# A gated cross-attention and ternary feed-forward block: another order of a step, token scales by one transpose, and another beginning

## The reference

```python
x = x + tanh(g_xattn) * attention(layernorm(x), ctx)          # 16 heads of 16, softmax over 128 keys
x = x + tanh(g_ffn) * ffn(layernorm(x))

def ffn(x):                        # D = 256, H = 1024
    h = bit_linear(x, w1)          # tokens rounded to 8 bits by their own maximum, weights ternary
    h = silu(depthwise_conv(h, conv_w, conv_b))   # 3 taps along the sequence, per feature
    return bit_linear(h, w2)
```

## Time and profile before

| | |
|---|---|
| median of 3 runs | 257.64 us (256.51 to 257.85) |
| profiled execution, its own time | 256.99 us |
| its span (first to last instruction) | 255.2 us |
| TensorE matmul busy | 217.7 us, 85% |
| VectorE busy | 200.0 us, 78% |
| ScalarE busy | 148.6 us, 58% |
| GpSimd busy | 123.1 us, 48% |
| mean granted clock of TensorE | 0.957 |

### The profile page before, as it was taken

One profiled execution on the slowest core, in us unless ns is written; L12 is line 12 of the kernel. 1 busy time (PEld: TensorE's weight loads), 2 busy tenths in 40 slices (PEclk: granted clock), 3 DMA queues, 4 the chain that ended last, 5 costly groups with the idle time before them and its releaser, 6 DMA issues.

```text
span 255.2 us, 6530 instructions
## 1 busy us (share of the span) xinstructions
PE 217.7 (85%) x2418; PEld 176.0 (69%) x2418; DVE 200.0 (78%) x414; ACT 148.6 (58%) x261; POOL 123.1 (48%) x227
## 2 busy tenths in 40 slices
PE   7577789889889999999999999989965886776874
PEld 7546677778778787777877877867744665665763
DVE  3123437989888479998988989879899999998971
ACT  0533664537446487676775866766763665666551
POOL 3302012472552747568586584653657524234360
PEclk9955999999999999999999999999995899999998
DMA  6951010110110101101000000000000000101011
GB/s 173 367 182 41 3 44 0 46 44 1 44 35 9 44 1 44 41 3 45 0 23 1 4 3 0 3 3 1 3 1 3 21 32 32 41 21 44 22 63 64
DMA packets 9489, 9.87 MB, mean 39 GB/s; under 512 B 1010, under 2 KB 9202, under 8 KB 9458
## 3 DMA queue, kind: packets, MB, share of 16 engines
q1 hardware_dynamic: 9458, 9.46, 11.5%
HBM read 7.36 MB, written 2.10 MB: 37 GB/s over the span
## 4 chain that ended last, share of the span: by engine, by line
PE 38%; DVE 21%; POOL 20%; issue 15%; ACT 5%; POOLq 0%; DVEq 0%; ACTq 0%
PE ps_score L410 5%; DVE zmax L948 5%; DVE smax L806 4%; POOL hid L310 4%; PE ps_max L420 4%; PE ps_proj L383 4%; PE ps_proj L375 3%; DVE y L862 3%; PE ps_av L434 3%; PE ps_proj L457 3%; DVE hid L855 3%; POOL xn L294 3%; PE ps_av L590 2%; PE ps_av L444 2%; DVE xres L958 2%
## 5 line engine op out<-in xcount | busy, mean ns | idle before, releaser
L806 DVE TENSOR_REDUCE smax<-ps_max 128x8 f32<-128x1024 f32 x32 | 39.2, 1224 | 28.5 <-PE ps_max L420 26.6
L652 ACT ACTIVATE prob<-ps_score 128x1024 f32<-128x1024 f32 x32 | 32.8, 1025 | 21.3 <-PE ps_score L410 20.8
L410 PE MATMUL ps_score<-Qs,KT 32*128 32x128 f32 x512 | 37.1, 282 | 8.2 <-ACT QT L647 6.2
L410 PEld LDWEIGHTS ps_score<-Qs,KT 32*128 32x128 f32 x512 | 31.7, 186 | 16.1 <-issue 15.2
L420 PE MATMUL ps_max<-KT,QT 32*128 32x256 f32 x256 | 38.1, 417 | 1.5 <-DVE smax L806 1.5
L681 ACT ACTIVATE y<-hid,conv 128x512 f32<-128x512 f32 x32 | 26.0, 813 | 7.9 <-DVE hid L855 7.1
L287 POOL TENSOR_SCALAR var<-mv 128x1 f32<-128x1 f32 x16 | 3.6, 224 | 52.5 <-DVE mv L837 52.5
L865 DVE SCALAR_TENSOR_TENSOR y<-hid,conv,y 128x508 f32<-128x508 f32 x32 | 25.5, 797 | 1.1
L862 DVE SCALAR_TENSOR_TENSOR y<-hid,conv,y 128x508 f32<-128x508 f32 x32 | 24.6, 768 | 0.9 <-ACT y L681 0.9
L420 PEld LDWEIGHTS ps_max<-KT,QT 32*128 32x128 f32 x256 | 22.9, 192 | 2.7 <-issue 2.4
L487 PE MATMUL ps_h<-xqT,w1q 128*128 128x512 bf16 x64 | 19.5, 388 | 1.1 <-ACT deq L668 0.7
(11 more groups left out here) (113 smaller groups left out, 519.9 us busy)
## 6 DMA issues: line engine op xcount, KB each, us to landing
cin<-ctxT SPq DMA_DIRECT2D x16, 128.0 KB, 2.1
xres<-x SPq DMA_DIRECT2D x16, 128.0 KB, 2.4
out<-xres SPq DMA_DIRECT2D x16, 128.0 KB, 1.7
w1f<-w1T SPq DMA_DIRECT2D x1, 1024.0 KB, 6.8
w2f<-w2T SPq DMA_DIRECT2D x1, 1024.0 KB, 9.2
wk<-wkT SPq DMA_DIRECT2D x1, 256.0 KB, 2.9
wv<-wvT SPq DMA_DIRECT2D x1, 256.0 KB, 4.2
wq<-wqT SPq DMA_DIRECT2D x1, 256.0 KB, 4.5
```

The lines of the kernel that those rows point to most:

```text
L410: mm = pe.matmul(ps_score[:, i * 512 + j * P:i * 512 + (j + 1) * P], KT[b % 3][rows, j * P:(j + 1) * P], Qs[rows, j * P:(j + 1) * P], star ...
L652: act.activation(prob[pair][:, :], ps_score[:, :], ACT.Exp, scale=DH ** -0.5).then_inc(exp_done, 1)
L806: dve.tensor_reduce(dst, ps_max[:, :].rearrange("p (g t e k) -> p g t e k", g=PG, t=KD, e=2), AX.X, ALU.max).then_inc(max_done, 1)
```

## The change

It has four parts.

1. TensorE's order in a step: `project_v(n)` comes before `weigh(a)` instead of late; `int_transpose` moves from before `weigh` to behind `max_transpose`; `unweighted_transpose(a)` moves behind `project_q(n)`. The column sums of w2 move from step 6 to step 7.
2. Token scales: GpSimd no longer builds `deq_diag`; TensorE transposes the column of scales, read 128 times, and the mean of the weights is multiplied in when ScalarE copies the result.
3. Other engines' order: ScalarE takes both middle taps directly behind the exponential. VectorE's first taps come before `shift_q`, `quantise1` comes earlier, and the second taps come before `normalise` and the second `row_max` instead of behind it. GpSimd rounds before it multiplies the hidden tile and normalises x. The statistics of x are no longer taken on VectorE but by two passes on ScalarE (a sum, then a sum of squares around the mean) and small instructions on GpSimd. The weights are made ternary one step later.
4. The beginning: ScalarE loads its table at once and copies x before K; V(0) is projected after the first row stages; the first row maximum of sequence 0 goes to ps_score instead of ps_max; both steps of x and V of sequence 1 are written out; a few matmuls without use (`keep_busy`) are put into gaps.

```diff
@@ GpSimd
+            def x_mean(i):
+                gp.wait_ge(total_done, i - 1)
+                gp.tensor_scalar(minus_mean[:, :], x_total[:, :], -1.0 / D, None, ALU.mult).then_inc(mean1_done, 1)
...
-                gp.wait_ge(qa_step, 3 * d + 3)
+                gp.wait_ge(qrec_done, d + 1)
+                wait(gp, xq_ready, d)
                 gp.tensor_scalar(xn2[:, :], xn2[:, :], qa[:, 2:3], ROUND, ALU.mult, ALU.add).then_inc(round_done, 1)
-                wait(gp, xq_ready, d)
                 gp.wait_ge(round_done, d + 1)
-                gp.tensor_scalar(deq_diag[:, :], ident[:, :], qa[:, 3:4], 1.0, ALU.mult, ALU.mult).then_inc(diag_done, 1)
-                gp.tensor_scalar(xq[:, :], xn2[:, :], -ROUND, 1.0, ALU.add, ALU.mult).then_inc(diag_done, 1)
+                gp.tensor_scalar(xq[:, :], xn2[:, :], -ROUND, 1.0, ALU.add, ALU.mult).then_inc(int_done, 1)
...
                 if seq(s - 2):
                     norm2(s - 2)
-                if seq(s + 2):
-                    norm1(s + 2)
+                    round1(s - 2)
                 for T in TILES.get(s, ()):
                     if on_gp(T):
                         dequantise(T)
-                if seq(s - 2):
-                    round1(s - 2)
+                if seq(s + 2):
+                    norm1(s + 2)
+                if seq(s + 3):
+                    gp.wait_ge(sh1_done, s + 3)
+                    x_mean(s + 3)
@@ TensorE
+        def first_max(n, pair):
+            return ps_score if n == 0 and pair == 0 else ps_max
...
-                pe.matmul(ps_deq, ones[:, :], deq_diag[:, :], start=True, stop=True).then_inc(xq_ready, 1)
+                pe.transpose(ps_deq, qa[:, 1:2].broadcast_to([P, P]), ident[:, :]).then_inc(xq_ready, 1)
...
                 if seq(d):
                     project_out(d)
-                if seq(d - 1):
-                    int_transpose(d - 1, min(tiles, default=0))
+                if seq(n):
+                    project_v(n)
                 if seq(a):
                     weigh(a)
                 if seq(n):
                     x_transpose(n)
-                if seq(b):
-                    max_transpose(b)
+                max_transpose(b)
+                if s == SUMS_STEP:
+                    w2_column_sums()
+                elif seq(d - 1):
+                    int_transpose(d - 1, min(tiles, default=0))
+                if seq(n):
+                    project_q(n)
+                if s == SUMS_STEP:
+                    int_transpose(d - 1, min(tiles))
                 if seq(a):
                     unweighted_transpose(a)
-                if 0 in tiles:
-                    w2_column_sums()
-                if seq(n):
-                    project_v(n)
-                    project_q(n)
+                between()
...
             project_k(0)
-            pe.wait_ge(wv_in, 16)
-            project_v(0)
             x_transpose(0)
+            keep_busy(3)
             pe.wait_ge(wq_in, 16)
             project_q(0)
             project_k(1)
             row_stage(-1, 0)
             row_stage(-1, 1)
+            x_transpose(1)
+            keep_busy(2)
+            pe.wait_ge(wv_in, 16)
+            project_v(0)
+            project_q(1)
+            max_transpose(0)
             pe.wait_ge(v_ones, 2)
-            step(0)
+            project_v(1)
+            row_stage(0, 0)
+            project_k(2)
+            keep_busy(2)
+            row_stage(0, 1)
@@ ScalarE
+            def sum_x(i):
+                act.wait_ge(x_in[i], 16)
+                wait(act, mean1_done, i - 2)
+                act.activation(unused[0][:, :], xres[:, i * D:(i + 1) * D], ACT.Identity,
+                               accum_out=x_total[:, :]).then_inc(total_done, 1)
+
+            def square_x(i):
+                act.wait_ge(mean1_done, i - 1)
+                wait(act, var1_done, i)
+                act.activation(unused[1][:, :], xres[:, i * D:(i + 1) * D], ACT.Square, bias=minus_mean[:, :],
+                               accum_out=x_squares[:, :]).then_inc(squares_done, 1)
...
-                act.activation(deq[:, d * P:(d + 1) * P], ps_deq, ACT.Copy).then_inc(xq_done, 1)
+                act.activation(deq[:, d * P:(d + 1) * P], ps_deq, ACT.Identity,
+                               scale=w_mean[:, 0:1]).then_inc(xq_done, 1)
...
                     exponent(a, 1)
-                if seq(d - 1):
-                    int_copy(d - 1)
                 extra(0)
-                if seq(a):
-                    u_copy(a)
-                if seq(n):
-                    x_copy(n)
-                if 0 in tiles:
-                    w2_sums_copy()
-                extra(1)
-                for T in last[1:2]:
+                for T in last:
                     middle_tap(T)
                 if seq(n):
                     v_copy(n)
+                if seq(n + 2):
+                    sum_x(n + 2)
+                if seq(n):
+                    x_copy(n)
+                if seq(a):
+                    u_copy(a)
+                if s == SUMS_STEP:
+                    w2_sums_copy()
+                if seq(d - 1):
+                    int_copy(d - 1)
+                extra(1)
+                if seq(n):
                     q_copy(n)
+                if seq(n + 1):
+                    square_x(n + 1)
@@ VectorE
-                if seq(n + 1):
-                    norm_stats1(n + 1)
-                if seq(b):
-                    shift_q(b)
                 for T in last[0:1]:
+                    outer_taps(T)
+                extra(0)
+                shift_q(b)
+                if seq(d):
+                    quantise1(d)
+                for T in last[1:2]:
                     outer_taps(T)
                 if seq(a):
                     normalise(a)
-                if seq(d):
-                    quantise1(d)
-                extra(0)
                 if seq(n):
                     row_max(n, 1)
                 for T in tiles[1:2]:
                     dequantise(T)
-                for T in last[1:2]:
-                    outer_taps(T)
                 extra(1)
```

More of the change, by code:

```diff
@@ L99, in build @@
         stats1 = sb("stats1", [P, 6])
+        x_total = sb("x_total", [P, 1])
+        minus_mean = sb("minus_mean", [P, 1])
+        x_squares = sb("x_squares", [P, 1])
+        unused = [sb(f"unused{i}", [P, D]) for i in range(2)]
         mv1 = sb("mv1", [P, 2])
@@ L364, in project_k @@
                 pe.wait_ge(c_in[n % CB], loaded(n))
-                wait(pe, v_done, n)
+                if n == 1:
+                    pe.wait_ge(k_done, 1)
+                else:
+                    wait(pe, v_done, n)
                 for t in range(KD):
@@ L372, in project_v @@
             def project_v(n):
-                wait(pe, k_done, n + 1 if n > 0 else 0)
+                pe.wait_ge(k_done, max(n + 1, 2))
+                if n == 1:
+                    pe.wait_ge(v_done, 1)
                 for k in range(KD):
@@ L403, in row_stage @@
                     pe.wait_ge(q_done, n + 1)
-                    wait(pe, max_done, NP * n + pair)
+                    if n > 0:
+                        pe.wait_ge(max_done, NP * n + pair)
+                into = first_max(n, 1 - pair)
                 for j in range(GH):
@@ L490, in hidden, with step @@
                 mm.then_inc(h_ready, 1)
-            def step(s):
+            def step(s, between=lambda: None):
                 b, n, a, d = s, s + 1, s - 1, s - 2
@@ L535, in y_transpose, with keep_busy @@
                 mm.then_inc(zT_ready, 1)
+            def keep_busy(count):
+                for i in range(count):
+                    pe.matmul(ps_av[:, 0:P], ident[:, :], ident[:, :], start=True, stop=True)
             pe.wait_ge(ident_done, 1)
-            for i in range(WARM):
-                pe.matmul(ps_av[:, 0:P], ident[:, :], ident[:, :], start=True, stop=True)
+            keep_busy(WARM)
             pe.wait_ge(wk_in, 16)
             project_k(0)
-            pe.wait_ge(wv_in, 16)
-            project_v(0)
             x_transpose(0)
+            keep_busy(3)
             pe.wait_ge(wq_in, 16)
@@ L555, in _, with weight_means @@
             step(1)
[L556 to L562 removed]
+            pe.wait_ge(wo_in, 16)
+            def weight_means():
+                pe.wait_ge(gate_done, 1)
+                pe.wait_ge(abs_done, 1)
+                for half in range(2):
+                    mm = pe.matmul(ps_setup[:, 2:4], ones[:, :], abs_sum[:, 2 * half:2 * half + 2],
+                                   start=(half == 0), stop=(half == 1))
+                mm.then_inc(sums_ready, 1)
+            step(2, weight_means)
             pe.wait_ge(mean_done, 1)
             pe.wait_ge(ident16_done, 1)
[L565 removed]
+            for s in range(3, SB + 2):
                 step(s)
@@ L733, in half @@
                                         accum_out=abs_sum[:, 2 * k + i:2 * k + i + 1])
-                    if first == 1 and k == 1:
+                    if i == 1 and k == 1:
```

(7 more changed lines are left out.)

112 lines of the change are left out of this document (63 added, 49 removed).

## The result

The changed kernel takes 253.07 us (median; 249.93 to 256.02 over 20 executions) where the kernel before takes 256.5 us (254.86 to 258.14). The ratio is 0.984, with an interval of 0.981 to 0.987: faster by 1.6%, about 4 us. Every ratio in this document leaves out the executions that took over 1.5% longer than the fastest of the same kernel, which is why it is not the quotient of the medians (0.987 here, 3.4 us). The forecast was 248.1 us, so the sign was right and the gain was forecast at more than twice its size. The profiled execution took 252.81 us, of which the span is 251.0.

The account below looks back on a forecast made before the run. TensorE was taken as the bound while attention and hidden tiles overlap, VectorE close behind and the bound with taps after the change. Terms -8.8 - 3.4 - 0.35 + 3.1 + 0.6 = -8.85 gave 248.1 us; range 240.5 to 254.

Parts of the forecast that it names:

- The end: Behind R(14), mainly step 15: one more wait for xn2 (+0.9), two multiplications of 0.14 fall away; +0.6 us.
- rival 2: In the beginning, the full clock is lost again as before: +5.3 us, 253.4 us in all; chance 0.18.
- Beginning: Up to step 0's second maximum: earlier table load and x copy, full clock kept by filled gaps; -8.8 us.
- Steps 1 to 5: Steps without taps: wait for Q's copy nearly covered, cheaper scales, ScalarE's passes in idle time; -3.4 us.
- Steps 6 and 7: Step 6 like steps 3 to 5 plus 0.15, step 7 a cycle of 11.4 us; together -0.35 us.
- Steps 8 to 14: Steps with taps: VectorE becomes the bound, waiting some 0.9 us for xn2; cycle 10.8 us, +3.1 us.
- Rivals 1: In steps with taps, TensorE stays the bound as xn2 comes in time: cycle 9.9, 240.9 us; chance 0.20.
- rival 3: On ScalarE, Square needs another table than Exp, two loads in each of 14 steps: about +12, 260 us; chance 0.05.

Follow-up runs that it names:

- 249.33: The changed kernel with VectorE's second pair of taps back behind normalise and dequantise, in step 15 only: 249.33 us, ratio 0.977.
- 254.21: The changed kernel with GpSimd's product for tile 18 ahead of its two rounding instructions in step 15: 254.21 us, ratio 0.993.
- 252.38: The changed kernel with ScalarE's copies reordered (copy of x first; copy of Q earlier in steps without tiles): 252.38 us, ratio 0.975.
- 254.4 us: The changed kernel without the seven filler matmuls between the first transposes and step 1: 254.4 us, ratio 0.993.

## Why the prediction was wrong

**"The end" is the step that failed.** It counted step 15 as one more step with taps, one wait for xn2 (+0.9) less two multiplications, +0.6. It cost 5.2. Step 15 differs from the steps before it in that TensorE has no next sequence to project, so a late normalise leaves it idle for 2.05 us, and then the granted clock is low through the transposes of y, the last scores and the output projection, on which VectorE hangs. The 5.2 are made up of 2.85 for the lower clock (1.6 in step 15, 1.24 in the second half of step 14), 0.8 for the place of the taps at full clock, and 1.57 that stay with the taps behind normalise. The 1.24 are a matter of the execution too: in four other traces nearly the same waits in step 14 brought no fall of the clock. The 1.57 are more than covered by the wait for xn2, which is there (0.90), and one tap that began while GpSimd's product for tile 18 ran, 1.72 us long where those around it take 0.71 to 0.75. I looked at that step on VectorE and GpSimd and not at what TensorE would have left to do in it.

That 253.07 lies near the 253.4 of rival 2 is luck: what rival 2 describes did not happen. And the errors of the other four terms cancel (-1.0, +1.5, +0.35 and -0.8), so that the end alone is left as the miss.

**Beginning, -8.8: right**, measured -9.8. The clock was 1.00 throughout, so rival 2 is out. That the fillers were what keeps it is not so: it stays without them.

**Steps 1 to 5, -3.4: too large**, measured -1.9. I costed ScalarE's two passes at nothing by its idle time, and named as their price, if they were not covered, up to 0.6 in front of the copy of x. They weren't covered: ScalarE's idle time lies ahead of the copy of V, which waits for the weighting, and the sum stands behind that wait. With the copies in another order steps 3 to 5 take 9.36, against the forecast 9.4; without it they took 9.83, which is 1.3 of the 1.5 missing us.

**Steps 6 and 7, -0.35: 0.0.** Step 6 (9.95, forecast 9.55) still has the wait of 0.28 for the copy of x; with ScalarE's other order it takes 9.76. The rest is not explained. Step 7 took 11.36, as forecast.

**Steps 8 to 14, +3.1: nearly right**, measured +2.3. The cycle was 10.69 for 10.8 and the wait 0.79 for 0.9. The mechanism holds: the power ended behind the second tap. The Trainium skill ("SBUF — State Buffer", "Who interferes with whom") has the two-input VectorE instruction and GpSimd's read exclude each other, and the trace agrees (1.05 beside taps, 0.57 without). What I passed over is in one clause of mine, that VectorE's loss of the statistics of x is already in the count. The count was right, but that loss is a cause of the wait: it lets the taps start on top of the power, and the part that was to relieve VectorE cost 0.45 us per step.

**Rivals 1 and 3.** TensorE was not the bound, with the second taps on the path; with them behind the maximum, and the statistics back, it is, at 9.64 (I had put it at 9.9). Two table loads stand in the trace, so rival 3 is out.

## What to carry to other kernels

Work taken off a busy engine can buy nothing if what follows it then starts on top of another engine's short, critical chain; look at what the freed time lets begin, and what that runs beside. Treat the first and last turn of a pipelined loop as steps of their own: what fills TensorE beside a wait in the middle turns is missing there, and the wait of 2.05 us then cost another 1.6 through the clock. Put work that nobody waits for behind the instruction that frees a buffer, not into the queue in front of it.

## What the runs showed of the hardware

- The granted clock is part of the spread. One program, the changed kernel, gave 249.93 to 256.02 us; the kernel with the tile-18 product first, with the same weak place, took 252.25 us at a mean clock of 0.986 and 256.19 at 0.957. With fillers there the executions lie within 0.8 us (249.73 to 250.53), all at 0.993.
- The same waits don't always bring a fall. Waits of 0.75 to 0.84 and 0.79 us in step 14 were followed by a granted clock of 0.50 in the changed kernel's trace and in the 248.7 us kernel's, and by none in four others (those of 249.33, 254.21, 252.38 and 254.4 us).
- After the low clock has come, a busy TensorE doesn't end it at once: in the trace of the 248.7 us kernel, with the statistics on VectorE, it was busy for 7.67 of the 8 us from 170 to 178 and stayed at 0.50.
- One execution took 404.13 us at a granted clock that is recorded as 1.00. Its matmuls were long all the same; groups by line of it, then of the changed kernel:

```profile
L429 PE MATMUL ps_score<-Qs,KT 32*128 32x128 f32 x512 | 67.9, 453 | 0.0
```

```profile
L440 PE MATMUL ps_score<-Qs,KT 32*128 32x128 f32 x512 | 38.1, 287 | 2.7 <-DVE smax L886 1.6 <-ACT QT L708 1.1
```

The cause stays open; the same kernel's other 11 executions (245.2 to 250.31) showed nothing of it.
